# Fewer edge groups summed by way of "sheets" in a graph layer: four sheets in place of five

## The reference, cut to what matters

```python
def _hconv(x, src, dst, ew, w1, b1, w2, b2, g, b):
    h = jax.nn.relu(x @ w1 + b1)
    msg = ew[:, None] * h[src]
    agg = jax.ops.segment_sum(msg, dst, num_segments=x.shape[0])
    h = agg @ w2 + b2
    return jax.nn.relu(_bn(h, g, b))
...
x = x + gnn(layernorm(x))      # two _hconv layers, batch norms, residual
x = x + ffn(layernorm(x))      # 8 experts of three 256x256 products, softmax gate
```

## Time and profile before

| | us |
|---|---|
| median of 3 runs (5254.63 to 5257.71) | 5256.29 |
| profiled execution, its span | 5228.2 |
| median less that span | 28.1 |
| gathers of layer 1, first to last start | 175.3 to 1779.0 |
| gathers of layer 2, first to last start | 1928.7 to 3397.0 |
| PE busy in the span | 4623.3 (88%) |
| DVE, ACT, POOL busy | 51%, 47%, 40% |

### The profile page before, as it was taken

One profiled execution on the slowest core, in us unless ns is written; L12 is line 12 of the kernel. 1 busy time (PEld: TensorE's weight loads), 2 busy tenths in 40 slices (PEclk: granted clock), 3 DMA queues, 4 the chain that ended last, 5 costly groups with the idle time before them and its releaser, 6 DMA issues. The chain is left out here.

```text
span 5228.2 us, 71544 instructions
## 1 busy us (share of the span) xinstructions
PE 4623.3 (88%) x25508; PEld 3800.6 (73%) x25508; DVE 2688.7 (51%) x6606; ACT 2435.6 (47%) x4218; POOL 2110.6 (40%) x2284
## 2 busy tenths in 40 slices
PE   6778888888999579888988988649999999999999
PEld 5667777666677467776666666548888888888888
DVE  7666666566333464522222222366666666666665
ACT  4655556666211263300000000057777777777777
POOL 1466666566666456666666666630000000000000
PEclk9889999999999789999999999779999999999999
DMA  5467777566755247876666666431111111001110
GB/s 155 148 210 271 243 240 245 188 211 217 236 198 201 77 141 268 277 243 218 218 219 205 226 212 224 131 96 25 30 28 33 33 33 33 24 26 33 33 28 15
DMA packets 546618, 770.23 MB, mean 147 GB/s; under 512 B 149720, under 2 KB 441411, under 8 KB 546262
## 3 DMA queue, kind: packets, MB, share of 16 engines
q1 hardware_dynamic: 328176, 382.01, 21.7%
q0 software_dynamic: 100944, 273.96, 16.4%
q10 hardware_dynamic: 117142, 109.65, 6.5%
HBM read 605.58 MB, written 147.26 MB: 144 GB/s over the span
## 5 line engine op out<-in xcount | busy, mean ns | idle before, releaser
L1106 PE MATMUL pf<-work 128*128 128x330 f32 (+4 forms) x3528 | 1251.9, 491 | 63.3 <-DMA work<-front 31.3
L1054 POOL DMA_INDIRECT wst<-h,src_col x1040 | 1000.3, 962 | 541.9 <-issue 275.0
L1106 PEld LDWEIGHTS pf<-work 128*128 128x128 f32 x3528 | 661.0, 197 | 402.2 <-issue 220.1
L2096 DVE TENSOR_TENSOR f_hl<-f_hf,f_hh 128x1024 fp32r<-128x1024 f32 (+1 forms) x400 | 479.7, 1199 | 636.3 <-ACT f_hf L1959 636.0
L1952 ACT ACTIVATE f_hh<-f_p,f_sh,f_sc 128x512 fp32r<-128x512 f32 (+1 forms) x800 | 571.7, 768 | 395.9 <-PE f_p L2194 394.5
L1273 ACT ACTIVATE ah<-agg 128x1024 fp32r<-128x1024 f32 (+1 forms) x50 | 51.8, 1037 | 1464.2 <-DVE agg L1420 1086.6
L1138 PEld LDWEIGHTS ps<-oh,wst 128*128 128x128 f32 x4160 | 543.4, 203 | 144.5 <-issue 99.6
L1138 PE MATMUL ps<-oh,wst 128*128 128x128 f32 x4160 | 560.7, 288 | 88.6 <-issue 55.1
L1054 POOL DMA_INDIRECT f_xr<-h,src_col x518 | 497.7, 961 | 282.8 <-issue 134.0
L1054 POOL DMA_INDIRECT f_u<-h,src_col x512 | 491.1, 959 | 260.5 <-issue 136.7
L1959 ACT ACTIVATE f_hf<-f_p,f_sh,f_sc 128x512 f32<-128x512 f32 (+1 forms) x800 | 572.5, 775 | 0.0
(11 more groups left out here) (285 smaller groups left out, 7648.0 us busy)
## 6 DMA issues: line engine op xcount, KB each, us to landing
work<-h SPq DMA_DIRECT2D x216, 512.0 KB
work<-front SPq DMA_DIRECT2D x50, 924.0 KB
front<-agg ACTq DMA_DIRECT2D x12, 3300.0 KB
work<-front SPq DMA_DIRECT2D x50, 756.0 KB
work<-front SPq DMA_DIRECT2D x50, 660.0 KB
work<-front SPq DMA_DIRECT2D x50, 580.0 KB
front<-agg ACTq DMA_DIRECT2D x8, 2600.0 KB
work<-front SPq DMA_DIRECT2D x25, 832.0 KB
```

Of the source, the lines that this page charges most:

```text
L1054: g.indirect_dma_start(G[t % R], None, h_dram[layer], bass.IndirectOffsetOnAxis(ap=src_col[:, col:col + 1], axis=0)).then_inc(ga[t % R], 16)
L1106: ins = g.matmul(pF[:, k, 0:count * w].rearrange("p (s c) -> p s c", c=w), HB[a % 2][0:r, n, k * P:(k + 1) * P], x, start=b == 0, stop=b = ...
L2096: g.tensor_tensor(hlo[l][q % 2][:, :, 0:nn], hf[l][:, :, 0:nn], hhi[l][q % 2][:, :, 0:nn].bitcast(fp32), ALU.subtract).then_inc(f_lo[l], 1)
```

## The change

The fifth sheet is dropped. The third loses its last group (one segment of two groups in place of three), the fourth one of its five segments, and the fourth is now made in layer 2 and used only there. `FRONT_C` and `HOT_Q` follow: the sheet's sums reach less far, and the hot tiles are spread over fewer steps.

```diff
     SHEETS = [(42, [(1, 22, 3), (1, 9, 3), (2, 6, 4), (1, 5, 4), (3, 4, 5), (1, 3, 5)]),
               (66, [(3, 5, 6), (1, 4, 6), (3, 4, 7)]),
-              (58, [(5, 3, 7)]),
-              (66, [(5, 3, 7)]),
-              (52, [(2, 2, 7), (6, 2, 8)])]
+              (58, [(4, 3, 7), (1, 2, 7)]),
+              (66, [(4, 3, 7)])]
-    MADE = [[3, 2, 1, 0], [4]]
-    USED = [[3, 2, 1, 0], [3, 2, 1, 0, 4]]
+    MADE = [[2, 1, 0], [3]]
+    USED = [[2, 1, 0], [2, 1, 0, 3]]
...
-    FRONT_C = [3, 4]
+    FRONT_C = [3, 3]
...
-    HOT_Q = [188, 48]
+    HOT_Q = [172, 44]
```

## The result

The changed kernel takes 5423.72 us (median of 4 executions, 5416.21 to 5438.23) against 5255.46 before; the ratio is 1.0323, with a 95% interval of 1.0305 to 1.0341.

A forecast was written before the change was run, and what follows sets the result against it. Gathers, at about 1.46 us each, were taken as the bound, not PE. The terms +93 - 18 + 117 - 1 - 4 = +187 on 5256 gave 5443 us, range 5370 to 5485.

The forecast's parts named there:

- The bound: Both layers' aggregates: gathers set the pace at about 1.46 us each, whatever PE's load.
- Rival A: PE is the bound: layer 1 falls 160 us, layer 2 114, time 4978; chance 0.06, between it and no change 0.07.
- The tax of 0.2 us: On each gather in both layers: POOL stops at group borders, waiting for late updates, at any load of PE.
- 64 gathers in layer 1, +93: Layer 1: 64 more gathers at 1.458 us each add 93 us.
- the eased hot stretch, -18: Layer 1, where hot tiles and units stand together: less crowding saves 18 us, bounds 0 and -47.
- 80 gathers in layer 2, +117 - 1: Layer 2: 80 more gathers at 1.462 us add 117 us; fewer hot tiles save 1.
- Index tables, -4: Before the first gather: tables need one block of 128, not two, saving 4 us, between 0 and -6.
- PE's loss of 313 us at nothing: PE loses 160 and 153 us of work in the two layers; costed at nothing, as it lies beside gathers.
- The lower clock: Layer 2: at clock 0.71 a PE step takes 5.6 us, still fitting 5.85 of gathers, so no cost.
- Rival B: Layer 1's hot tiles and units also go at 1.458, long stretches at 1.44: +130 us, 5386; chance 0.18.
- The ends, at nothing: Ends of both layers: last units 12 and 20 steps before the end as before, same products, no change.
- Rival C: More crowding: added gathers cost 1.53 us in layer 1, 1.484 in layer 2, +217, 5473; chance 0.11.

The follow-up runs named there:

- the other direction: Kernel before, changed the other way: four more sheet groups in each layer, eight gathered groups fewer; 5194.26 us against 5219.76, ratio 0.9943.
- thin units: Kernel before with about three quarters of the sheets' product on PE left out, batches, hot tiles and gathers kept; 5262.22 us against 5257.69, ratio 1.0012.
- thin hot products: Kernel before with PE's hot products cut to 64 columns and DVE adding only eight blocks of each part, handovers kept; 5256.54 us, ratio 1.0008.
- layer 2's part alone: Kernel before with only the fifth sheet cut, from eight segments to two, layer 1 unchanged; 5331.03 us against 5252.21, ratio 1.0149.
- twelve buffers: Kernel before with 12 gather buffers in place of 16; 5254.19 us against 5257.69, ratio 0.9988.
- same-chip profile: Second profile of the unaltered changed kernel, on the chip that ran the kernel with thin hot products; measured 5417.76 us.

## Why the prediction was right, point by point

- **The bound: right.** Gathers, not PE. It was read from three paces alike at three loads of PE, and three runs settle it: PE's work left out gives nothing, gathers left out give 459 us, the other direction is faster. Rival A is refuted in full and in half.
- **The tax of 0.2 us: right in size, and its picture incomplete.** I called it a stop that comes back at any load. The runs show the size of it: 1.43 us for each gather, of which POOL's row and the gap behind it hold 1.25 (0.95 + 0.30), and the stop makes up the rest. The Trainium skill says why POOL's row is short (Perfetto Trace Analysis, DMA Instruction — SWDGE (GPSIMD)): the recorded end is the end of making the descriptors, not of the transfer. The trace agrees: the last gather of the group of the earlier trace rows starts at 3329.95, its row ends 0.94 us later, and PE, idle until its rows are there, starts at 3332.68. What the Trainium skill says there doesn't explain the 1.43. That the updates queue behind the gathers in some common path is a reading, and which path it is, no run shows; where POOL never stops, PE also stands before matmuls that wait for nothing, which a late update doesn't explain.
- **64 gathers in layer 1, +93, and the eased hot stretch, -18.** The sum of the two, 75, stands against 82 on the same chip, and 91 and 105 against before's profile. The mis-sized term is the -18: from 345 to 1300 the changed kernel has 617 and 626 gathers in its two profiles, the kernel before 623. That is 0 within 9 us, and the runs with thin units and thin hot products show why: less work on PE or DVE doesn't ease that stretch. My lower bound, 0 by the hot tiles' own chain between DVE and PE, had the right value. The chain's work is refuted as the reason; its handovers are not, and stay open.
- **80 gathers in layer 2, +117 - 1: right**, 115 and 118 against before's profile, 109 on the same chip.
- **Index tables, -4:** it is -9, beyond my bound of -6, and -7.4 with layer 2's part alone; on the same chip -8. That PE's and ACT's work on the second block goes too would explain it, but is only argued.
- **PE's loss of 313 us at nothing: right.** The units' line has 2744 matmuls, as forecast. PE's share in the long stretch is 81%, not 75%: the clock fell to 0.87 and the same work takes longer. The lower clock cost nothing in the time, as argued: with thin units it was 0.75, at the same pace.
- **Rival B has a remnant.** On one chip the long stretch goes at 1.472 with all batches (thin hot products, 659 gathers from 2230 to 3200) and at 1.463 and 1.461 in the two kernels with fewer (663 and 664). With 1.472 the 80 gathers of layer 2 would have cost 118 there and not 109. The other profiles agree. In the same window thin units and twelve buffers have 1.476 (all batches), and the first profile of after 1.459. The median turn of twelve gathers is 17.55 to 17.57 in the three profiles with all batches and 17.49 to 17.52 in the three with fewer, which also have more such turns (40 to 43 against 28 to 32). Before's own 1.462 doesn't speak against it: its turn of twelve is 17.38, as in the kernels on the chip where before takes 5220 (17.36 and 17.38), so its paces and those of after may be of two chips. If it is real, it is the batches' transfers and not PE's products, which the thin units left out without effect; no run left out batches alone.
- **The ends, at nothing:** by the same-chip profile they aren't quite. The stretch between the layers is 4 us shorter and the one behind the last gather 12 us, of which I know no cause.
- **The sum: 187 for 168.** On one chip it is 167: -8 + 82 - 4 + 109 - 12 for my -4 + 75 + 0 + 116 + 0. So the layers' parts are right to 7 us each, with opposite signs, and what is too high lies in the stretches outside the gathers. That the sum of the layers (191 for 191) comes out so well is luck in part. By the first pair of profiles the whole is 188 and 208, because before's profiled execution lay some 26 us under its median. The prediction lays the 28.1 us "around" its span; the profile after shows 1.8 there. The rest, 10 us in layer 1 and 8 in layer 2 against the same-chip profile, is that of the execution or of its chip. Rival C's 217 leaves out the 4 us of the index tables; with them it is 213 and 5469. Nothing hangs on it.

## What to carry to other kernels

An engine that is 90% busy need not be the bound: divide stretches with different loads of it by the number of items, and see whether the pace changes. The row of an indirect DMA on its engine isn't its price; count the time from stop to stop over the gathers in it, here 1.43 us for 128 rows or for 64. Halving the rows saved nothing; whether a gather of more than 128 would cost the same, no run shows. A step that costs gathers can be traded against matmuls that lie under them until the other engine's work fills the step, here at 4.93 us of 5.85.

## What the runs showed of the hardware that I had not expected

- While gathers are issued without a stop (1.40 us each), PE's products reach DVE 8.7 us late (at least 7.9 in all 80 cases), while DVE's updates reach PE in 0.15 us, and PE stands up to 3.2 us before matmuls that wait for nothing. Behind the gathers all of it is gone. Taking a wait away made the kernel 40% slower.
- A gather of 64 rows costs as much as one of 128: 17.40 and 17.36 us for twelve.
- One chip ran the kernel before in 4850 us, the others in 5220 to 5258. All forecasts here hold for chips of the second kind, and among these the turn of twelve gathers still differs by 1% (17.36 and 17.55 us).
- The execution that was profiled can lie 26 us from the median, and two profiles of the changed kernel lie 20 us apart (5436.4 and 5415.9): a difference of 10 us between two single profiles of 5200 us tells nothing.
